# Where the experts' weights are split into rounded part and rest: in the last attention step, or piece by piece in steps 2 to 21 with both parts kept in DRAM

## What is computed

```python
def step(carry, kvq):
    W, b = carry
    k, v, q = kvq
    g = 2.0 / d_h * (W @ k + b - v)
    W = W - LR * jnp.outer(g, k)
    b = b - LR * g
    return ((W, b), W @ q + b)
...
x = _layernorm(x + attn(x))
shared = silu(x @ sW1 + sb1) @ sW2 + sb2
activation = sqrt(softplus(x @ routing_W.T + expert_bias))
top_vals, top_idx = jax.lax.top_k(activation, 2)
hdn = silu(einsum('nd,edh->enh', x, rW1) + rb1)      # 8 experts, h = 256
y = einsum('enh,ehd->end', hdn, rW2) + rb2
x = _layernorm(x + shared + einsum('ne,end->nd', combine, y))
```

## Time and profile before

| | |
|---|---|
| median of 3 runs | 2428.95 us (2425.66 to 2430.55) |
| span of the profiled execution | 2423.3 us |
| TensorE (PE) busy | 2266.6 us, 94% |
| VectorE (DVE) busy | 1544.1 us, 64% |
| ScalarE (ACT) busy | 918.8 us, 38% |
| GpSimd (POOL) busy | 1185.2 us, 49% |
| share of the 16 DMA engines, queue of SP / of POOL | 18.3% / 8.5% |
| mean granted TensorE clock | 0.974 |

### The profile page before, as it was taken

The page is one execution under the profiler, slowest core; times in us unless marked ns, Lnnn a source line. Parts: engine busy times, 40 slices in busy tenths (PEclk is TensorE's granted clock), DMA queues, the critical chain, the costliest instruction groups (busy, mean ns, idle before and its releaser), DMA issues.

```text
span 2423.3 us, 40797 instructions
## 1 busy us (share of the span) xinstructions
PE 2266.6 (94%) x13218; PEld 1962.0 (81%) x13218; DVE 1544.1 (64%) x3622; ACT 918.8 (38%) x1979; POOL 1185.2 (49%) x1120
## 2 busy tenths in 40 slices
PE   8999999999999999999999999997579879999886
PEld 7888888888888888888888888886568768888775
DVE  5666655566655776666666676657345334888798
ACT  4333333333333333333333332323444334545444
POOL 1344333344333336544445543456555555777777
PEclk9999999999999999999999999998789899999998
DMA  4111111111111111111111111103423324887896
GB/s 163 36 38 41 44 40 48 35 36 44 44 40 49 36 36 44 36 44 40 45 40 36 44 42 38 45 18 101 160 92 126 99 83 158 281 281 238 274 329 217
DMA packets 100285, 220.52 MB, mean 91 GB/s; under 512 B 20835, under 2 KB 21475, under 8 KB 99313
## 3 DMA queue, kind: packets, MB, share of 16 engines
q1 hardware_dynamic: 71856, 150.65, 18.3%
q0 software_dynamic: 27936, 67.22, 8.5%
q10 hardware_dynamic: 288, 0.04, 0.0%
HBM read 142.54 MB, written 86.39 MB: 94 GB/s over the span
## 4 chain that ended last, share of the span: by engine, by line
PE 78%; DVE 11%; issue 5%; ACT 2%; DMA 1%; another core or an unknown queue 1%; POOL 1%; DVEq 1%; SPq 0%; ACTq 0%; POOLq 0%
PE banks L115 23%; PE banks L117 22%; PE banks L116 22%; PE banks L121 6%; PE banks L759 2%; DVE xc L1149 2%; DVE b_Y L1149 1%; PE banks L496 1%; DVE b_XL L1146 1%; DVE b_small L1710 1%; PE banks L786 1%; PE banks L534 1%; PE banks L592 1%; DVE b_Y L1146 1%
## 5 line engine op out<-in xcount | busy, mean ns | idle before, releaser
L115 PE MATMUL banks<-W 128*128 128x512 f32 (+1 forms) x2040 | 751.8, 369 | 9.9 <-DVE W L1146 8.0
L117 PE MATMUL banks<-W 128*128 128x512 f32 (+1 forms) x2040 | 717.7, 352 | 0.0
L116 PE MATMUL banks<-W 128*128 128x512 f32 (+1 forms) x2040 | 715.4, 351 | 0.0
L115 PEld LDWEIGHTS banks<-W 128*128 128x128 f32 x2040 | 387.4, 190 | 57.6 <-issue 8.5
L117 PEld LDWEIGHTS banks<-W 128*128 128x128 f32 x2040 | 386.4, 189 | 54.9
L116 PEld LDWEIGHTS banks<-W 128*128 128x128 f32 x2040 | 388.0, 190 | 46.5
L1767 POOL TENSOR_TENSOR W<-S,W 128x512 fp32r<-128x512 f32 (+1 forms) x256 | 332.4, 1324 | 117.2 <-ACT W L830 116.5
L830 ACT ACTIVATE W<-banks 128x512 fp32r<-128x512 f32 x320 | 190.9, 597 | 522.1 <-DVE banks L1146 227.7
L1767 POOL TENSOR_TENSOR X<-X,B 128x1024 f32<-128x1024 f32 x32 | 76.7, 2396 | 584.6 <-DMA X<-in_x 584.5
L830 ACT ACTIVATE W<-S 128x512 fp32r<-128x512 f32 (+1 forms) x276 | 173.3, 651 | 231.9 <-DVE S L1146 213.1
L115 PE MATMUL banks<-W,b_XL 128*128 (+1 forms) x644 | 201.0, 312 | 31.7 <-issue 20.7
(11 more groups left out here) (168 smaller groups left out, 4499.4 us busy)
## 6 DMA issues: line engine op xcount, KB each, us to landing
RG<-ys SPq DMA_DIRECT2D x128, 256.0 KB
XT<-in_xT SPq DMA_DIRECT2D x32, 512.0 KB
X<-in_x SPq DMA_DIRECT2D x32, 512.0 KB, 3.5
x1d<-X SPq DMA_DIRECT2D x64, 256.0 KB
out<-b_Y SPq DMA_DIRECT2D x64, 256.0 KB
zd<-X SPq DMA_DIRECT2D x52, 256.0 KB, 2.0
b_Y<-zd SPq DMA_DIRECT2D x52, 256.0 KB
S<-in_we SPq DMA_DIRECT2D x20, 256.0 KB, 5.6
```

The lines of the kernel that those rows point to most:

```text
L115: e.matmul(o, ll, rh, start=start, stop=False, skip_group_check=True)
L116: e.matmul(o, lh, rl, start=False, stop=False, skip_group_check=True)
L117: return e.matmul(o, lh, rh, start=False, stop=stop, skip_group_check=True)
```

## The change

GpSimd now splits the weights early. In step t of `PRESPLIT` (2 to 13 and 18 to 21) it does two quarters (`presplit`): a copy that rounds and a subtraction, each 128x512, between its residual additions of the step and `xb`. SyncE loads these quarters into the buffer `RG` at the end of step t-1 and stores each with both parts (512 KB) into a DRAM tensor `wd`. `RG` is also the router's memory; the router of a group starts when the stores are through, and the quarters from step 18 on are loaded after the first routing. At the end of step 0 the split weights of the shared expert are stored to `wd` as well (2 MB). In the last step 16 plain DMAs of 1 MB bring both parts into `W`; the splits of ScalarE, VectorE and GpSimd in and behind step 31 are gone, and the shared expert comes back with one DMA of 2 MB at item 133 instead of four quarters and their splits.

```diff
+PRESPLIT = [*range(2, 14), *range(18, 22)]
-def load_weights(k, e, w, m):
...
-    w.wait_ge(*k.d_w.of(m - 8))
-    e.dma_start(weight_home(k, m)[2], k.a["we"][x, :, q * D:(q + 1) * D]).then_inc(k.d_w.sem(m), 16)
+def load_weights(k, e, w, n):
+    for m in (4 * E - 2, 4 * E - 1):
+        w.wait_ge(*k.d_wo.of(m))
+    home_free(k, w, n)
+    w.wait_ge(*k.d_w.of(n - 8))
+    x, j = divmod(n, 2)
+    e.dma_start(f32(k.W[:, n * 2048:(n + 1) * 2048]), k.wd[x][:, j * 2048:(j + 1) * 2048]).then_inc(k.d_w.sem(n), 16)
 def weights_ready(k, w):
+    for s, v in k.d_w.last(2 * E):
+        w.wait_ge(s, v)
...
+def state_done(k, w):
+    w.wait_ge(k.s_Shi, 8 * (k.NT - 1))
+    w.wait_ge(k.s_Slo, 8 * (k.NT - 1))
...
 # gpsimd
+    def presplit(m):
+        hi, raw, _ = staged(k, m)
+        w.wait_ge(*k.d_wr.of(m))
+        e.tensor_copy(hi.bitcast(F32R), raw).then_inc(k.s_wh, 1)
+        w.wait_ge(k.s_wh, m + 1)
+        tt(raw.bitcast(F32R), raw, hi, ALU.subtract).then_inc(k.s_wl, 1)
...
+        for m in split_pair(t):
+            presplit(m)
         scattered = scatters(t)
         next(scattered, None)
         xb(t)
...
-            for m in (0, 3, 6, 8):
-                split_w(m)
...
-    for m in (11, 14, 16, 19, 22, 24, 27):
-        split_w(m)
-    load(0)
-    load(1)
-    split_w(30)
-    load(2)
-    load(3)
+    for i in range(4):
+        load(i)
...
 # sync
+        if t == 0:
+            keep_shared()
+        for m in split_pair(t + 1):
+            load_quarter(m)
         if t == NT - 2:
-            for m in range(4, 12):
-                load_weights(k, e, w, m)
...
+            for n in range(2):
+                load_weights(k, e, w, n)
         store_z(t, 0)
+        for m in split_pair(t + 1):
+            store_quarter(m)
         store_z(t, 1)
         load_x(t + 1)
...
+    for n in range(2, 15):
+        load_weights(k, e, w, n)
...
+    def shared_again():
+        w.wait_ge(k.d_we, 64)
+        w.wait_ge(k.s_dn, k.plan.again)
+        e.dma_start(f32(k.W[:, 0:WC]), k.wd[E]).then_inc(k.d_again, 16)
...
-        if i in k.plan.stage:
-            load_again(k.plan.stage[i])
-        if i == k.plan.again + 14:
+        if i == k.plan.again + 3:
+            shared_again()
             biases_again()
```

More of the change, by code:

```diff
@@ L384, in plan_of @@
     k.items, p.finals = [], []
-    p.again, p.stage = c["slot"] + c["tiles"], {}
+    p.again = c["slot"] + c["tiles"]
     p.buffer, p.before, holder, base = {}, {}, {}, 0
@@ L396, in plan_of @@
             k.items.append(g)
-            if (i - p.again) % 3 == 1 and 0 <= i - p.again < 12:
-                q = (i - p.again) // 3
-                x = min(range(RING), key=lambda x: free[x])
-                free[x], p.stage[i] = i + 6, q
-                p.buffer["stage", q], p.before["stage", q], holder[x] = x, holder.get(x), ("stage", q)
         x = min(range(RING), key=lambda x: free[x])
@@ L415, in plan_of @@
     p.M = N + c["tiles"]
-    assert sorted(p.stage.values()) == list(range(4))
     p.base = {f.base: c for c, f in enumerate(p.finals)}
@@ L770, in up @@
         else:
-            w.wait_ge(k.s_shlo, 7)
+            w.wait_ge(k.d_again, 16)
         for dc in range(KC):
@@ L993, in scalar_program @@
             k_proj(n, 0)
-        else:
-            for m in range(4):
-                split_w(m)
         if t > 0:
@@ L1100, in scalar_program @@
             load_ids(k, e, w, k.groups[1 if i == 32 else 2])
-def again(k, q):
-    hi, lo, _ = weight_home(k, q)
-    return hi, lo, k.Y[k.plan.buffer["stage", q]][:]
 def load_ids(k, e, w, g):
@@ L1368, in route @@
         w.wait_ge(k.s_wt, wt_before(k, x))
+        for s, v in k.d_wo.last(2 * len([t for t in PRESPLIT if t < g["step"] + g["steps"]])):
+            w.wait_ge(s, v)
         stepped(tt(Z, k.LG[:, 0:T, :], row(bias), ALU.add))
@@ L1858, in gpsimd_program @@
         next(scattered, None)
-        if not more:
-            for m in (0, 3, 6, 8):
-                split_w(m)
         o_part(t, 0)
```

167 lines of the change are left out of this document (45 added, 122 removed).

## The result

The changed kernel takes **2411.25 us** (median of 6 runs, 2401.29 to 2412.79), the kernel before in the same comparison 2428.3 us (6 runs, 2420.1 to 2430.55). The ratio is **0.9926, 95% interval 0.9907 to 0.9946**: faster by 0.74%. Forecast were 2410.0 us and a range of 2402 to 2426. The profiled execution has a span of 2410.5 us against 2423.3, 12.8 us less.

A forecast was written before the change was run, and what follows sets the result against it. PE was taken as the bound in steps and most items, idling in the last step; VectorE and full DMA engines bound the end. Gains 17.9 + 0 + 1 = 18.9 us from 2428.95 gave 2410.0 us, range 2402 to 2426.

The forecast's parts named there:

- The weights: Last step: 18.6 MB through the queue at 400 GB/s, first item at 1702.3 instead of 1720.2, 17.9 us less.
- The tokens: Last step: gather issued at about 1690, first item possible at 1697 to 1702, just inside the weights.
- the bound of 8 us for the first: Last step: the first gather, beside a full queue, was allowed 3.7 to 8 us to land.
- the first item waits for the tokens: Rival, start of items: gathers land only when the queue empties, about 7 us of gain lost, 2417 us; chance 0.10.
- Step 31's own chain: Last step: chain ends some 2 us earlier, 0 to 4 us put on it for loads, still before the weights.
- The steps: Attention steps: GpSimd's early splits fit in its wait for X, cost taken as 0, bounds 0 and 13 us.
- the rival of 13 us: Attention steps: presplit meets VectorE, 16 steps pay 0.8 us each, 2423 us; chance 0.12.
- The end: Near item 134: scalings save 4.1 us, added load costs 2.9; 1 us gained taken, bounds 4 gained, 3 lost.
- The burst: Near item 134: 2 MB at once, its additional 1 MB costing 2.9 us of full DMA engines.
- The sum: Whole kernel: 17.9 + 0 + 1 = 18.9 us less, span 2404.4, median 2410.0 us.
- The 5.65 us that the prediction laid around the span: Whole kernel: time outside the profiled span, 5.65 us, assumed to stay unchanged.

The follow-up runs named there:

- all the repairs together: Changed kernel with shared-expert load in eight pieces, early tokens, four weight loads ahead of X, last step-30 scatters deferred, up weights first; 2399.7 us, ratio 0.9894 to kernel before.
- the three repaired kernels: Changed kernel with eight 256 KB loads and four weight loads before X (0.9916); plus early tokens and deferred scatters (0.9916); plus up weights first (0.9894).
- e5: Changed kernel unaltered, timed again beside the kernel before: 2319.0 us against 2338.8, ratio 0.9916.
- e9: Kernel before, unaltered, run again for its profile: 2425.3 us beside its own median of 2422.8.
- the run of the four repairs: Changed kernel with eight 256 KB loads, early tokens, four weight loads before X, step-30 state splits before scatters; 2324.1 us, ratio 0.9937 to kernel before.

## Why the prediction was right, point by point

**The weights** (-17.9 us in the sum): right in the result and, in its parts, by errors that cancel. Start 1651.8 against 1652.4; the gap at `X` 1.6 us against 1.0 (3 us with 201 GB/s where 424 could go); rate 422 to 424 GB/s against 400. By the rate alone 18.6 MB would have taken 44.0 us and not 46.5. But by the rates of the stretches some 20 MB went through from 1651 us until PE could start. The biases and the stores of `x1d`, issued from 1685.35 on, can be among them; the trace doesn't say whose bytes they were. PE's last wait for nothing visible was 0.34 us, not 1.0. The item stood at 1702.49 against 1702.3.

**The tokens**: the issue at about 1690 was right (1690.30), and so was the bound of 8 us for the first; the second item's gather took 9.2. That was the part I left out. PE transposes the second item's tokens ahead of the first item's product, so the second landing counts. The rival "the first item waits for the tokens" came true at a price of under half a microsecond, because weights and tokens arrived together; the prediction had named 1702.3 and 1697 to 1702 for them.

**Step 31's own chain**: the chain was to end 2 us earlier and pay up to 4 us for the loads beside it. With half the bytes it was 3.7 us shorter, so it paid at least that. I had named the scatters, but not that they delay a split of the state and through it VectorE. It did not decide, as forecast: with the weights there in time, the start would be at +49 to +50.

**The steps**: zero was right, and the rival of 13 us is refuted, even for twice the work. The rounding copy took 0.61 us, within its bounds. GpSimd's wait for `X` was 17.31 us where about 18 was forecast.

**The end** is the step that failed: -1 us was forecast. The three scalings of 1.90 us beside the shared expert's splits do go, and the 4.1 us were gained: the lead grows by 1.4 us at each of the three. (Two more, beside the late items' residual additions, stand in both kernels and change nothing. Here is the first of them, in the kernel before and in the changed one.)

```profile
2361.54 1.90 DVE L1717 TENSOR_SCALAR b_Y<-b_Y,b_small 128x512 f32<-128x512 f32 x1
2348.81 1.89 DVE L1653 TENSOR_SCALAR b_Y<-b_Y,b_small 128x512 f32<-128x512 f32 x1
```

The burst was put at 2.9 us for its additional megabyte, and VectorE's wait for rows at 3 us at most. It was 7.3, and 5.7 to 7.6 in four further profiles of kernels with that load. The price was taken from the bytes, where it follows from the order in the queue. The rows of the next final were asked for 3.5 us behind the load and reached VectorE 14.2 us after that (2277.46 to 2291.66), at 384 GB/s; with the load in eight pieces the longest wait was 0.9 us. In the first profile the term was a loss of 3.8 us: the lead falls from 16.56 us at item 137 (2294.70 against 2278.14) to 12.73 at item 160.

**The sum**: by the spans the change gave 12.8 us where 18.9 were forecast. Of the 6.1 us that are missing, the end accounts for 4.8 (a loss of 3.8 for a gain of 1.0). The rest lies in the items before it, where the lead swings, from 17.8 us at item 16 to 14.4 at item 24 and back to 16.6, with waits put down to issue and remote in either kernel. By the medians the change gave 17.1 us, and 19.9 on the lower level. The 5.65 us that the prediction laid around the span were mostly scatter: a run's time is about 2 us above its own span (2412.35 against 2410.5). The forecast of 2410.0 hit 2411.25 with some luck: by the spans it was 6.1 us off, and the two kernels' runs scatter by 10 us on this level.

## What to carry to other kernels

When several conditions for one start are within a few microseconds of each other, removing one shows only the next. Here half the bytes gave 5 us, earlier tokens nothing, earlier weights nothing, all the repairs together 4 in the start of the first item. A large load in front of small ones on the same queue costs the wait of whoever needs the next small one. Price it by what is queued ahead at that moment, and cut it into pieces of the size that the consumers' spacing can hide. And before an instruction is moved behind something, read what stands behind its new place.

## What the runs showed of the hardware

- Two levels of time for the same kernel: 2423 to 2428 us and 2337 to 2339. The attention steps are alike to 0.1 us on both (52.02 us a step); all of the difference lies in the items' stage, 690 to 708 us against 608 to 617. On the upper level VectorE's waits put down to issue and remote sum to 93 us in one profile of the changed kernel, 73 and 76 us in the two of the kernel before, 69 to 94 in the three repaired kernels, and 1.4 to 2.8 us in the eight profiles on the lower level. I had not expected it; what these waits are is not shown, and no run here was made for it. The comparisons of e5 (lower) and e9 (upper) both name chip 1, so the chip's number doesn't tell the level.
- One queue of plain 1 MB loads, with other traffic beside it, brought the DMA engines to 422 to 424 GB/s for nearly 40 us. That is above the 358 GB/s that the Trainium skill (DMA: Bandwidth & Descriptors, "Bandwidth") names as the bound of the HBM side. It agrees with the 425 GB/s that the same section has for 16 MB on one core with the pair's other core idle.
- Behind such a queue a 256 KB gather issued by GpSimd took 9.2 us instead of the 3.7 of the kernel before, and in the run of the four repairs two scatters in a row, each waiting for the one two before it, waited 3.6 to 4.8 us together.
- A scaling of VectorE, or its `MM<-xc,smallc` (1660.10 + 1.28 + 0.29 = 1661.67, its end), that meets a 128x512 subtraction or addition of GpSimd ended 0.28 to 0.31 us behind GpSimd's end in each case looked at. Not every instruction does: the split `b_XL<-banks,b_XH` at 2359.40 in the changed kernel ran its usual 0.68 us beside such an addition (2358.96 to 2360.24).
